# A graph attention kernel: edge features turned by DVE instead of TensorE, and eight output places in the last stage

## The chip, the cores and the metric

The kernel runs on one core of one Trainium2 chip. The metric is the device time of one execution in microseconds (us); lower is better. Engines carry the names of the profile: PE (TensorE), DVE (VectorE), ACT (ScalarE), POOL (GpSimd) and SP (SyncE).

## The reference

N = 12500 nodes with 96 features, 8 heads of 12, E = 412500 edges sorted by destination. Each edge has 96 features of its own.

```
q = x @ Wq + bq;  k = x @ Wk + bk;  v = x @ Wv + bv      # per node
e = edge_attr @ We + be                                  # per edge
score = k[src] * q[dst] / sqrt(12) * e                   # per edge, 96 wide
score = exp(clip(score summed over each head, -5, 5))    # per edge and head
wV = segment_sum(v[src] * score, dst);  Z = segment_sum(score, dst)
out = layernorm(x + wV / (Z + 1e-6))
```

## The kernel before, in words

The edges are taken in C = 806 chunks of 512 (CHUNK), each as G = 4 tiles of 128. There are four stages.

*Nodes.* 25 batches of 4 x 125 nodes: PE turns x and multiplies it, and the rows of k and v go to a table in DRAM, `kv_table`, 768 bytes a node; then 25 batches for q, stored in three bf16 parts in `q_table`, while DVE clears `accT`, which holds the sums of all nodes (L874). Tables of the destinations are turned on PE (L590) and copied by DVE (L850).

*Main stage.* Each engine runs a step of its own for each chunk, all in a loop written out eight or sixteen steps at a time, and they meet by counting semaphores only:
- POOL (L518 to L531) waits until the place of its ring is free (`msg_ready` of 8 chunks before, RING = 8) and issues 4 indirect gathers of `kv_table` rows (L527), whose row numbers come from `src_idx`.
- PE (L616 to L654), in step s: four turns of `ea` of chunk s (L635, edges by features into features by edges), with the products with `w_e` of chunk s - 2 between them (L637), the selection of query rows of chunk s - 2 (L644), and the sums of chunk s - 5 (L651); then it adds one to `pe_step`. Float32 products are issued as two passes each. Each product has two places in PSUM.
- ACT (L758 to L778) waits for `pe_step` s + 1: the exponential of the scores (L764), the copy of the turned edges to SBUF as `eaT` (L767), two operations that make the selection matrix `ohT` (L772, L775), and in every fourth step a load of source numbers (L340).
- DVE (L885 to L929) waits for `pe_step` a + 3: it multiplies gathered keys with queries (L898) and with e (L906), makes the matrix `oh` (L901), the messages (L910), which release POOL, the sums over heads (L917), adds to `accT` (L925) and clips the scores (L929).
- SP (L387 to L395), every 4 chunks, waits for `pe_step` (L390) and loads `ea` (L371), the destinations `dst_b` (L384) and four windows of queries (L379).

*Last stage.* 25 batches: PE turns the sums back (L703), DVE divides (L992, L995, L1000), POOL adds x (L549), DVE takes mean and variance (L1006, L1020), ACT the root, DVE its reciprocal (L1011) and the shift, minus mean times that (L1016), ACT applies both, SP stores. The finished rows have four places; the division (L1000) waits until the store of four batches before is done.

Of the kernel before, what the change touches and what calls it, by code (L numbers as in the profile page):

```python
# [20 lines left out]
PROJ_LAG = 2  # L21
SUM_LAG = 5
SEL = WIN * PARTS
SEL_READ = 106
RING = 8
HALF = RING // 2
IDX_RING = 16
# [14 lines left out]
def run_steps(engine, step, chunks, lag, round_values=None, from_round=0, unroll=RING, ahead=0):  # L42

    rounds = (chunks - 1 - ahead) // unroll
    if from_round == 0:
        for s in range(unroll):
            step(s, s, None)
# [8 lines left out]
def run_batches(engine, step, batches, lag, shift=0, after_first=None, before_last=None):  # L56

    rounds = (batches - 1 - shift) // 4
    for b in range(4 + shift):
        step(b, b % 4)
    if after_first is not None:
        after_first()
    with engine.Fori(1, rounds) as i:
        for u in range(4):
            step(i * 4 + u + shift, (u + shift) % 4)
    if before_last is not None:
        before_last()  # L70
    for b in range(rounds * 4 + shift, batches + lag):
        step(b, b % 4)


def gnn_kernel(nc, x, src, dst, edge_attr, Wq, bq, Wk, bk, We, be, Wv, bv, out):
# [14 lines left out]
    assert NQ * NJ == FULL and FULL == C - 1 and NP * TILES == N and DUP % G == 0  # L90
# [3 lines left out]
    assert CHUNK <= 512 and BATCH * max(DZ, NP) <= 512 and NQ * G <= 512 and BATCH % 2 == 0  # L94
# [7 lines left out]
    with ExitStack() as ctx:  # L102
# [3 lines left out]
        def sem(name):  # L106
# [13 lines left out]
        x_in = sb("x_in", [P, 4, BATCH, D])  # L120
        kv_out = sb("kv_out", [P, 4, BATCH, 2 * D])
        q_rest = sb("q_rest", [P, 2, BATCH, D])
        q_out = sb("q_out", [P, 4, BATCH, PARTS, D], BF16)
# [4 lines left out]
        spare = sb("spare", [P, 2 * 4 * BATCH * D + 2 * BATCH * D])  # L128
        dst_nat = spare[0:NQ, 0:NJ * CHUNK]
        dst16 = sb("dst16", [NQ, NJ * CHUNK], I16)  # L130
        dst16_end = sb("dst16_end", [1, CHUNK], I16)
        dst_end_row = sb("dst_end_row", [1, CHUNK], I32)
        dst_end = sb("dst_end", [P, G], I32)
        lohi = sb("lohi", [P, 4, NJ])
# [8 lines left out]
        rel = sb("rel", [P, C * G])  # L143

        ea = sb("ea", [P, RING, G, D])
# [3 lines left out]
        kv = sb("kv", [P, RING, G, 2 * D])  # L149
        eaT = sb("eaT", [DA, 2, CHUNK])  # L150
        away = sb("away", [SEL, CHUNK], BF16)
        ohT = sb("ohT", [SEL, 2, CHUNK], BF16)
        oh = sb("oh", [P, 2, G, WIN])
# [3 lines left out]
        msg = sb("msg", [P, 2, G, DZ])  # L157
# [5 lines left out]
        x_res, y = [spare[:, lo * BATCH * D:hi * BATCH * D].rearrange("p (u j d) -> p u j d", j=BATCH, d=D)  # L163
                    for lo, hi in ((0, 4), (4, 8))]
# [9 lines left out]
        eaT_ps, e_ps, q_ps, sum_ps = bank[0:2], bank[2:4], bank[4:6], bank[6:8]  # L174
# [5 lines left out]
        ones_ready = sem("ones_ready")  # L180
        w_kvq_in = sem("w_kvq_in")
        w_e_in = sem("w_e_in")
        dst_in = sem("dst_in")
        ends_in = sem("ends_in")
# [30 lines left out]
        ea_in = [sem(f"ea_in{i}") for i in range(2)]  # L215
        dst_b_in = [sem(f"dst_b_in{i}") for i in range(2)]
        q_win_in = [sem(f"q_win_in{i}") for i in range(RING)]
        src_idx_in = [sem(f"src_idx_in{i}") for i in range(IDX_RING // IDX_GROUP)]
# [4 lines left out]
        eaT_copied = sem("eaT_copied")  # L223
# [17 lines left out]
        f_eaT_copied = sem("f_eaT_copied")  # L241
# [27 lines left out]
        std_inverted = sem("std_inverted")  # L269
        coef_ready = sem("coef_ready")  # L270
        y_ready = sem("y_ready")
        y_stored = [sem(f"y_stored{i}") for i in range(4)]
# [53 lines left out]
        def wait_batch(engine, sems, b, u):  # L326

            engine.wait_ge(sems[u], 32 * (b // 4 + 1) if isinstance(b, int) else (b - u) * 8 + 32)
# [6 lines left out]
        def load_sources(engine, s, u):  # L335

            count = max(0, min(IDX_GROUP, C - s)) if isinstance(s, int) else IDX_GROUP
# [710 lines left out]
```

## Time and profile before

| | |
|---|---|
| median of 3 runs | 5354.8 us (5341.96 to 5366.8) |
| profiled execution: its time, its span | 5346.04 us, 5344.1 us |
| mean granted PE clock of it | 0.508 of full speed |
| busy share of the span: PE, DVE, ACT, POOL | 67%, 39%, 31%, 59% |
| main stage, last stage | about 235 to 5235 us, 5235 to 5344 us |

Busy time is time in which an instruction of the engine ran; the idle time before it is put down to what ended it. "remote" means that the releaser is not in the profile. PEld is PE's loading of weights, which overlaps its matmuls.

### The profile page before, as it was taken

Reading aid. Unit: us, or ns where it says so; the run is one execution under the profiler, and the core shown is the slowest. Engines: PE = TensorE matmul, PEld = TensorE weight load, DVE = VectorE, ACT = ScalarE, POOL = GpSimd, SP = SyncE. Lnnn points to the kernel's source line nnn. Section 1 sums busy time; section 2 is a strip of 40 time slices with the busy share of each in tenths; the row PEclk is TensorE's granted clock in tenths of the full one; section 3 lists DMA queues with packets and bytes.
Section 4 is the critical chain, followed back from the end, with each engine's and each line's share of the span. In section 5 each row is a group of like instructions: output and inputs, shape, how many; then the busy total and the mean of one; then the engine's idle time right before and its main releaser. Section 6 shows DMA issues by size and latency. Waiting matters only on the chain.

```text
span 5344.1 us, 72613 instructions
## 1 busy us (share of the span) xinstructions
PE 3563.7 (67%) x19972; PEld 3430.0 (64%) x19973; DVE 2070.6 (39%) x6072; ACT 1676.7 (31%) x3477; POOL 3154.1 (59%) x3274
## 2 busy tenths in 40 slices
PE   7666666666666666666666666666666666666665
PEld 6666666666666666666666666666666666666664
DVE  4433333333333333333333343333333333333336
ACT  4323232333323332323332332333322323333234
POOL 4566565565665656555656566655566565665662
PEclk7555555555555555555555555555555555555555
DMA  7344444444444444444444444444444444444443
GB/s 227 107 110 118 110 109 109 109 118 110 109 111 113 115 109 110 118 110 108 110 113 113 109 108 110 114 113 109 109 110 119 108 112 112 114 109 108 110 117 91
DMA packets 497769, 607.51 MB, mean 114 GB/s; under 512 B 256053, under 2 KB 420224, under 8 KB 497630
## 3 DMA queue, kind: packets, MB, share of 16 engines
q0 software_dynamic: 155200, 318.39, 22.6%
q1 hardware_dynamic: 233215, 281.36, 18.0%
q10 hardware_dynamic: 109330, 7.48, 1.5%
q8 instruction: 10, 0.16, 0.0%
q14 instruction: 14, 0.11, 0.0%
HBM read 584.51 MB, written 22.46 MB: 114 GB/s over the span
## 4 chain that ended last, share of the span: by engine, by line
PE 46%; issue 25%; another core or an unknown queue 18%; DVE 6%; DVEq 2%; ACT 1%; DMA 1%; SPq 1%; ACTq 0%; POOL 0%; POOLq 0%
PE bank L637 16%; PE bank L651 15%; PE bank L635 10%; PE bank L644 4%; DVE kqe L906 2%; DVE raw_score L917 1%; DVEq L298 1%; DVE oh L901 1%; DVE kqe L898 0%; ACT eaT L767 0%; DMA out_dram<-spare 0%; ACT spare L805 0%; DVE msg L910 0%; DVE accT L925 0%
## 5 line engine op out<-in xcount | busy, mean ns | idle before, releaser
L527 POOL DMA_INDIRECT kv<-kv_table,src_idx x3224 | 3104.5, 963 | 2090.2 <-DVE msg L910 1041.2
L637 PE MATMUL bank<-w_e,eaT 97*128 97x96 f32 x6448 | 1882.9, 392 | 216.6 <-issue 216.6
L635 PE MATMUL bank<-ident,ea 128*96 128x128 f32 x3224 | 1355.3, 421 | 958.3 <-issue 517.5
L637 PEld LDWEIGHTS bank<-w_e,eaT 97*128 97x128 f32 x6448 | 1776.7, 334 | 222.8 <-issue 221.9
L898 DVE TENSOR_TENSOR kqe<-kv,bank 128x384 f32<-128x384 f32 x806 | 446.6, 554 | 3179.6 <-remote 2432.5
L651 PE MATMUL bank<-oh,msg 128*104 128x32 f32 x6448 | 1284.8, 353 | 276.7 <-issue 273.5
L635 PEld LDWEIGHTS bank<-ident,ea 128*96 128x96 f32 x3224 | 806.0, 250 | 986.2 <-issue 515.0
L651 PEld LDWEIGHTS bank<-oh,msg 128*104 128x104 f32 x6448 | 1234.3, 289 | 269.0 <-issue 264.9
L764 ACT ACTIVATE msg<-score 128x32 f32<-128x32 f32 x806 | 184.8, 229 | 3523.9 <-remote 2569.5
L644 PEld LDWEIGHTS bank<-q_win,ohT 96*128 96x128 bf16 x3224 | 401.4, 155 | 338.8 <-issue 332.4
L644 PE MATMUL bank<-q_win,ohT 96*128 96x96 bf16 x3224 | 447.2, 279 | 245.5 <-issue 241.1
L772 ACT ACTIVATE away<-dst_b,minus_id 96x512 bf16<-96x512 int16 x806 | 581.1, 721 | 0.0
L775 ACT ACTIVATE ohT<-away 96x512 bf16<-96x512 bf16 x806 | 508.1, 630 | 25.5
L767 ACT COPY eaT<-bank 96x512 f32<-96x512 f32 x806 | 454.1, 563 | 4.9 <-PE bank L644 4.2
L910 DVE TENSOR_TENSOR msg<-kv,msg 128x384 f32<-128x384 f32 x806 | 443.3, 550 | 0.2 <-ACT msg L764 0.2
L906 DVE TENSOR_TENSOR kqe<-kqe,bank 128x384 f32<-128x384 f32 x806 | 440.1, 546 | 0.0
L917 DVE TENSOR_REDUCE raw_score<-kqe 128x32 f32<-128x384 f32 x806 | 438.1, 544 | 0.0
L901 DVE TENSOR_TENSOR oh<-iota,rel 128x128 f32<-128x128 f32 x806 | 230.7, 286 | 0.0
L929 DVE TENSOR_SCALAR score<-raw_score 128x32 f32<-128x32 f32 x806 | 185.4, 230 | 0.1
L925 DVE TENSOR_TENSOR accT<-bank,accT 104x32 f32 x806 | 144.3, 179 | 2.8 <-PE bank L651 2.3
L549 POOL TENSOR_TENSOR spare<-spare 125x384 f32<-125x384 f32 x25 | 25.0, 1000 | 77.6 <-DVE spare L1000 77.6
L703 PE MATMUL bank<-ident,accT 104*125 104x104 f32 x100 | 30.6, 464 | 41.5 <-DVE spare L1000 39.1
(78 smaller groups left out, 481.0 us busy)
## 6 DMA issues: line engine op xcount, KB each, us to landing
ea<-in_edge_attr_dram SPq DMA_DIRECT2D x201, 768.0 KB
dst_b<-dst_by_chunk SPq DMA_DIRECT2D x201, 384.0 KB
kv<-kv_table,src_idx POOLq DMA_INDIRECT x3224
q_win<-q_table SPq DMA_DIRECT2D x806, 19.9 KB
kv_table<-kv_out SPq DMA_DIRECT2D x25, 336.0 KB
q_table<-q_out SPq DMA_DIRECT2D x25, 252.0 KB
spare<-in_x_dram SPq DMA_DIRECT2D x25, 168.0 KB
out_dram<-spare SPq DMA_DIRECT2D x25, 168.0 KB
```

Of the source, the lines that this page charges most:

```text
L527: pool.indirect_dma_start(kv[:, slot, g, :], None, kv_dram[:, :], bass.IndirectOffsetOnAxis(ap=src_idx[:, u, g:g + 1], axis=0)).then_inc(k ...
L635: last = nc.tensor.transpose(eaT_ps[u % 2][0:D, g * P:(g + 1) * P], ea[:, u, g, :], ident[:, :])
L637: nc.tensor.matmul(e_ps[v % 2][:, g * D:(g + 1) * D], eaT[:, v % 2, g * P:(g + 1) * P], w_e[:, :], start=True, stop=True)
L644: last = nc.tensor.matmul(q_ps[v % 2][:, g * D:(g + 1) * D], sel[:, g, :], q_win[0:SEL, v, :], start=(g == 0), stop=(g == G - 1), skip_gro ...
L651: last = nc.tensor.matmul(sum_ps[w % 2][0:DZ, 0:WIN], msg[:, w % 2, g, :], oh[:, w % 2, g, :], start=(g == 0), stop=(g == G - 1))
L767: nc.scalar.copy(eaT[0:D, u % 2, :], eaT_ps[u % 2][0:D, :]).then_inc(eaT_copied, 1)
L772: nc.scalar.activation(away[:, :], dst_b[:, u % RING, :], ACT.Abs, bias=minus_id[:, bass.ds(s, 1)]).then_inc(away_done, 1)
L775: nc.scalar.activation(ohT[:, u % 2, :], away[:, :], ACT.Relu, bias=1.0, scale=-1.0).then_inc(ohT_built, 1)
L898: nc.vector.tensor_tensor(kqe[:, :, :], kv[:, ua, :, 0:D], q_ps[ua % 2][:, 0:G * D].rearrange("p (g d) -> p g d", g=G), ALU.mult).then_inc ...
L906: nc.vector.tensor_tensor(kqe[:, :, :], kqe[:, :, :], e_ps[ua % 2][:, 0:G * D].rearrange("p (g d) -> p g d", g=G), ALU.mult).then_inc(kqe_ ...
L910: nc.vector.tensor_tensor(msg[:, um % 2, :, 0:D].rearrange("p g (h d) -> p g h d", d=HD), kv[:, um, :, D:2 * D].rearrange("p g (h d) -> p ...
L917: nc.vector.tensor_reduce(raw_score[:, :], kqe[:, :, :].rearrange("p g (h d) -> p (g h) d", d=HD), AX_X, ALU.add).then_inc(heads_summed, 1)
```

## The change

Edge features. `ea` is no longer turned by PE and copied by ACT. A load of 4 chunks becomes three loads, one for each 32 of the 96 features. Each puts edge 32 b + i of its block b on partition i, so that 32 features of one edge (128 bytes in DRAM) are one piece. That is 2048 pieces for each of the three loads, where one load had 512 pieces of 1536 bytes. On DVE one instruction per chunk turns the 32x32 blocks of 96x512 into `eaT`. These loads have a ring of 16 chunks, are issued by ACT and go 15 chunks ahead. The order of edges inside a chunk changes with it, in all tables alike.

Pipeline. `eaT`, `ohT`, `oh`, `msg` and the PSUM results have four places (DEPTH = 4). PE's step s now works on chunk s for both products, and on chunk s - 5 for the sums. DVE's turn and ACT's `ohT` are made 4 steps ahead. DVE waits for `pe_step` a + 1.

Tables. All source numbers are loaded once and turned on PE (28 small turns) and copied by DVE to `src_tab`; ACT copies 4 chunks of them every fourth step in place of the load. The destination tables' turns are spread over the node batches. `dst_b` is loaded by ACT, x by SP, the numbers of the edges by POOL. In the query stage every second clearing of `accT` (12 of 25) is made by ACT.

Last stage. The finished rows have eight places. The shift is made by POOL in two operations of 125x4 (zero minus mean, times the reciprocal), behind its own addition of x.

The diff, cut to its core:

```diff
+        def load_edges(engine, s, g):
+
+            count = min(EA_GROUP, C - s) if isinstance(s, int) else EA_GROUP
             whole = count - 1 if isinstance(s, int) and s + count == C else count
-            if whole > 0:
-                engine.dma_start(src_idx[:, u:u + whole, :], src[bass.ds(s * CHUNK, whole * CHUNK)].rearrange(
-                    "(c p g) -> p c g", p=P, g=G)).then_inc(src_idx_in[u // IDX_GROUP], 16)
-            if whole < count:
-                engine.dma_start(src_idx[:, u + whole, :], src[E - CHUNK:E].rearrange(
-                    "(p g) -> p g", g=G)).then_inc(src_idx_in[u // IDX_GROUP], 16)
+            parts = [(s * CHUNK, g * EA_GROUP, whole)] + ([(E - CHUNK, g * EA_GROUP + whole, 1)] if whole < count else [])
+            for edge, slot, chunks in parts:
+                for k in range(0, D, SQ):
+                    engine.dma_start(ea[k:k + SQ, slot:slot + chunks, :].rearrange("i c (b f) -> i (c b) f", f=SQ),
+                                     edge_attr[bass.ds(edge, chunks * CHUNK), k:k + SQ].rearrange(
+                                         "(b i) f -> i b f", i=SQ)).then_inc(ea_in[g], 16)
...
             def half_round(s, h, bases):
 
-                sp.wait_ge(pe_step, s - HALF + PROJ_LAG)
+                sp.wait_ge(pe_step, s - HALF)
                 sp.sem_inc(loads_allowed, 1)
-                load_edges(s, h)
-                load_destinations(s, h)
...
+            def finish(b, u):
+                if not isinstance(b, int) or b < BATCHES:
+                    pool.wait_ge(y_attended, b + 1)
+                    wait_batch(pool, x_res_in, b, u % 4)
+                    nc.gpsimd.tensor_tensor(y[0:NP, u, :, :], y[0:NP, u, :, :], x_res[0:NP, u % 4, :, :], ALU.add).then_inc(res_added, 1)
+                if not isinstance(b, int) or b >= 2:
+                    w = u % 2
+                    pool.wait_ge(std_inverted, b - 1)
+                    nc.gpsimd.tensor_tensor(shift[0:NP, w, :], zero[0:NP, 0:1].to_broadcast((NP, BATCH)), mean_var[0:NP, w, :, 0],
+                                            ALU.subtract).then_inc(mean_negated, 1)
+                    pool.wait_ge(mean_negated, b - 1)
+                    nc.gpsimd.tensor_tensor(shift[0:NP, w, :], shift[0:NP, w, :], std_inv[0:NP, w, :], ALU.mult).then_inc(coef_ready, 1)
+
+            run_batches(pool, finish, BATCHES, 2, 0, OUT_RING)
...
-                if projecting:
-                    pe.wait_ge(eaT_copied, c + 1)
-                    at_least(pe, kqe_done, c - 1)
-                for g in range(G):
-                    if turning:
-                        last = nc.tensor.transpose(eaT_ps[u % 2][0:D, g * P:(g + 1) * P], ea[:, u, g, :], ident[:, :])
...
+                if projecting:
+
+                    pe.wait_ge(ea_turned, s + 1)
+                    for g in range(G):
+                        nc.tensor.matmul(e_ps[v][:, g * D:(g + 1) * D], eaT[:, v, g * P:(g + 1) * P],
...
+            def copy_sources(s, u):
+
+                count = max(0, min(IDX_GROUP, C - s)) if isinstance(s, int) else IDX_GROUP
+                if count > 0:
+                    nc.scalar.copy(src_idx[:, u:u + count, :], src_tab[:, bass.ds(s * G, count * G)].rearrange(
+                        "p (c g) -> p c g", g=G)).then_inc(src_copied, count)
...
-                    nc.scalar.copy(eaT[0:D, u % 2, :], eaT_ps[u % 2][0:D, :]).then_inc(eaT_copied, 1)
...
+                    if w % HALF == HALF - 1 and (not isinstance(t, int) or t + HALF + 1 < C):
+                        load_destinations(act, t + HALF + 1, w // HALF)
+
+                if u % IDX_GROUP == 0 and (not isinstance(s, int) or s >= 0):
+                    copy_sources(s + IDX_AHEAD, (u + IDX_AHEAD) % IDX_RING)
+
+                if u % EA_GROUP == 1 and (not isinstance(s, int) or 0 <= s and s + EA_AHEAD < C):
+                    act.wait_ge(ea_turned, s + EA_AHEAD - EA_RING + EA_GROUP)
+                    load_edges(act, s + EA_AHEAD, (u + EA_AHEAD) % EA_RING // EA_GROUP)
...
-                dve.wait_ge(pe_step, a + PROJ_LAG + 1)
...
+                    dve.wait_ge(pe_step, a + 1)
...
+                    w = (u + DEPTH) % EA_RING
+                    if w % EA_GROUP == 0:
+                        landed_edges(dve, t, w)
+                    nc.vector.transpose(eaT[0:D, v, :], ea[:, w, :]).then_inc(ea_turned, 1)
...
-                    if not isinstance(b, int) or b >= 4:
-                        wait_batch(dve, y_stored, b - 4, u)
+                    if not isinstance(b, int) or b >= OUT_RING:
+                        wait_batch(dve, y_stored, b - OUT_RING, u)
...
-                    nc.vector.scalar_tensor_tensor(shift[0:NP, w, :], mean_var[0:NP, w, :, 0], -1.0, std_inv[0:NP, w, :],
-                                                   ALU.mult, ALU.mult).then_inc(coef_ready, 1)
```

PE, one step of the main loop. Before, the turn into one PSUM bank alternates with the product into another:

```order
L631 REGISTER_ALU
L635 MATMUL bank1<-ident,ea 96x128
L637 MATMUL bank3<-w_e,eaT 128x96
L635 MATMUL bank1<-ident,ea 96x128
L637 MATMUL bank3<-w_e,eaT 128x96
L635 MATMUL bank1<-ident,ea 96x128
L637 MATMUL bank3<-w_e,eaT 128x96
L635 MATMUL bank1<-ident,ea 96x128
L637 MATMUL bank3<-w_e,eaT 128x96
L644 MATMUL bank5<-q_win,ohT 128x96 x4
L651 MATMUL bank6<-oh,msg 104x32 x4
```

After, two steps; the turns are gone and each chunk has its own bank out of four:

```order
L663 REGISTER_ALU
L665 MATMUL bank1<-w_e,eaT 128x96 x4
L670 MATMUL bank5<-q_win,ohT 128x96 x4
L678 MATMUL bank1<-oh,msg 104x32 x4
L663 REGISTER_ALU
L665 MATMUL bank2<-w_e,eaT 128x96 x4
L670 MATMUL bank6<-q_win,ohT 128x96 x4
L678 MATMUL bank2<-oh,msg 104x32 x4
```

The four L635 rows left the step, and the sums (L678) share a bank with the products of e (L665).

DVE, one step of the main loop. Before, the step ends with the clipping of the scores:

```order
L898 TENSOR_TENSOR kqe<-kv,bank5 128x384
L901 TENSOR_TENSOR oh<-iota,rel 128x128
L906 TENSOR_TENSOR kqe<-kqe,bank3 128x384
L910 TENSOR_TENSOR msg<-kv,msg 128x4x96
L917 TENSOR_REDUCE raw_score<-kqe 128x32
L922 TENSOR_LOAD base_tab
L922 ISA x2
L925 ISA
L925 TENSOR_TENSOR accT<-bank6,accT 104x32
L929 TENSOR_SCALAR score<-raw_score 128x32
```

After, with the lines of the changed kernel:

```order
L944 TENSOR_TENSOR kqe<-kv_mem,bank4 128x384
L947 TENSOR_TENSOR oh<-iota,rel 128x128
L952 TENSOR_TENSOR kqe<-kqe,bank0 128x384
L956 TENSOR_TENSOR msg<-kv_mem,msg 128x4x96
L963 TENSOR_REDUCE raw_score<-kqe 128x32
L968 TENSOR_LOAD base_tab
L968 ISA x2
L971 ISA
L971 TENSOR_TENSOR accT<-bank0,accT 104x32
L975 TENSOR_SCALAR score<-raw_score 128x32
L980 STREAM_TRANSPOSE eaT<-ea_mem 96x512
```

One row was added, the turn at the step's end, for the chunk four steps ahead.

ACT, in the main loop. Before, the step with the load of source numbers at its end:

```order
L764 ACTIVATE msg<-score 128x4x8
L767 COPY eaT<-bank0 96x512
L285 ISA
L772 ISA
L772 ACTIVATE away<-dst_b,minus_id 96x512
L775 ACTIVATE ohT<-away 96x512
L340 ISA
L340 DMA src_idx<-in_src_dram 128x4x4
L760 REGISTER_ALU
```

After, the steps around the two kinds of loads (`ea_mem` holds the edge features, `src_tab` the source numbers):

```order
L376 DMA dst_b<-dst_by_chunk 96x2048
L791 ACTIVATE msg<-score 128x4x8
L798 ACTIVATE away<-dst_b,minus_id 96x512
L801 ACTIVATE ohT<-away 96x512
L757 CAST src_idx<-src_tab 128x16
L791 ACTIVATE msg<-score 128x4x8
L798 ACTIVATE away<-dst_b,minus_id 96x512
L801 ACTIVATE ohT<-away 96x512
L361 DMA ea_mem<-in_edge_attr_96_dram 32x64x32 x3
```

The copy of `eaT` and the source load left ACT; a small copy, one load of destinations and three loads of edge features per four steps came to it.

## Rows read from the trace of the kernel before

**Rows 1.** Stretch of the main stage: PE, PEld, DVE, ACT, POOL busy (count), clock, DMA share, GB/s.
```profile
2235.00:3235.00 1000.00, 666.51 (x3754) 644.78 (x3754) 377.85 (x1092) 304.70 (x624) 601.55 (x626) 0.50 0.41 111
```

**Rows 2.** Groups by line, main stage: busy, mean ns, idle time before and releasers.
```profile
L527 POOL DMA_INDIRECT kv<-kv_table,src_idx x3132 | 3011.9, 962 | 1988.9 <-DVE msg L910 1000.0 <-issue 988.8
```

**Rows 3.** Timeline of GpSimd: start, duration, operation, idle time before.
```profile
2483.27 0.95 POOL L527 DMA_INDIRECT kv<-kv_table,src_idx  x1 [4.83 <-DVE msg L910]
...
2508.68 0.95 POOL L527 DMA_INDIRECT kv<-kv_table,src_idx  x1 [4.67 <-DVE msg L910]
2509.93 1.14 POOL L527 DMA_INDIRECT kv<-kv_table,src_idx  x1 [0.30 <-issue]
```

**Rows 4.** Timeline of DVE, the same 26 us.
```profile
2486.41 0.55 DVE L898 TENSOR_TENSOR kqe<-kv,bank 128x384 f32<-128x384 f32 x1 [0.75 <-PE bank L651]
...
2496.78 0.56 DVE L898 TENSOR_TENSOR kqe<-kv,bank 128x384 f32<-128x384 f32 x1 [8.00 <-remote]
...
2506.18 0.55 DVE L898 TENSOR_TENSOR kqe<-kv,bank 128x384 f32<-128x384 f32 x1 [7.01 <-remote]
...
2508.56 0.55 DVE L898 TENSOR_TENSOR kqe<-kv,bank 128x384 f32<-128x384 f32 x1
...
2511.77 0.55 DVE L898 TENSOR_TENSOR kqe<-kv,bank 128x384 f32<-128x384 f32 x1 [0.69 <-PE bank L651]
```

**Rows 5.** Chain of waits in order of time: start, length, what.
```profile
2486.38 0.24 PE bank L635
...
2486.99 0.21 PE bank L635
...
2490.43 0.24 PE bank L635
...
2494.48 3.68 issue
...
2501.39 1.79 issue
```

**Rows 6.** Page, costliest groups: who waits for "remote".
```profile
L898 DVE TENSOR_TENSOR kqe<-kv,bank 128x384 f32<-128x384 f32 x806 | 446.6, 554 | 3179.6 <-remote 2432.5
...
L764 ACT ACTIVATE msg<-score 128x32 f32<-128x32 f32 x806 | 184.8, 229 | 3523.9 <-remote 2569.5
```

**Rows 7.** Waits of SyncE's queue: total us, times, longest.
```profile
SPq L390 <- remote: 2135.8, 130, 23.9
```

**Rows 8.** Timeline of all engines around the first gather.
```profile
67.64 2.08 SPq L384 DMA_DIRECT2D dst_b<-dst_by_chunk  x2
...
71.30 1.05 POOL L527 DMA_INDIRECT kv<-kv_table,src_idx  x1 [32.23 <-DMA kv_table<-kv_out]
...
80.28 7.03 PE L601 MATMUL bank<-w_kvq,accT 97*125 97x96 f32 x32 [7.03 <-issue]
```

**Rows 9.** Page, costliest groups: the rows that the edits touch.
```profile
L527 POOL DMA_INDIRECT kv<-kv_table,src_idx x3224 | 3104.5, 963 | 2090.2 <-DVE msg L910 1041.2
...
L635 PE MATMUL bank<-ident,ea 128*96 128x128 f32 x3224 | 1355.3, 421 | 958.3 <-issue 517.5
...
L549 POOL TENSOR_TENSOR spare<-spare 125x384 f32<-125x384 f32 x25 | 25.0, 1000 | 77.6 <-DVE spare L1000 77.6
```

**Rows 10.** Timeline of DVE in the last stage.
```profile
5285.17 0.56 DVE L1000 TENSOR_TENSOR spare<-bank,z_inv 125x384 f32<-125x384 f32 x1 [1.01 <-DMA out_dram<-spare]
...
5287.70 0.56 DVE L1000 TENSOR_TENSOR spare<-bank,z_inv 125x384 f32<-125x384 f32 x1
...
5289.08 0.28 DVE L1016 SCALAR_TENSOR_TENSOR shift<-mean_var,std_inv 125x4 f32<-125x4 f32 x1
```

**Rows 11.** Waits in the last stage: total us, times, longest.
```profile
DVE spare L1000 <- DMA out_dram<-spare: 14.0, 16, 1.8
```

**Rows 12.** Page, DMA queues: packets, bytes, share of 16 engines' span.
```profile
q1 hardware_dynamic: 233215, 281.36, 18.0%
q10 hardware_dynamic: 109330, 7.48, 1.5%
```

More of the change, by code:

```diff
@@ L39, in at_least, with run_steps @@
         engine.wait_ge(sem, value)
-def run_steps(engine, step, chunks, lag, round_values=None, from_round=0, unroll=RING, ahead=0):
+def run_steps(engine, step, chunks, lag, round_values=None, lead=0, unroll=RING, ahead=0):
     rounds = (chunks - 1 - ahead) // unroll
-    if from_round == 0:
-        for s in range(unroll):
-            step(s, s, None)
+    for s in range(-lead, unroll):
+        step(s, s % unroll, None)
     with engine.Fori(1, rounds) as i:
@@ L53, in run_steps, with run_batches @@
         step(s, s % unroll, None)
[L56 to L65, printed above, removed]
-    with engine.Fori(1, rounds) as i:
[L67 to L72, printed above, removed]
+def run_batches(engine, step, batches, lag, shift=0, unroll=4):
+    rounds = (batches - 1 - shift) // unroll
+    for b in range(unroll + shift):
+        step(b, b % unroll)
+    with engine.Fori(1, rounds) as i:
+        for u in range(unroll):
+            step(i * unroll + u + shift, (u + shift) % unroll)
+    for b in range(rounds * unroll + shift, batches + lag):
+        step(b, b % unroll)
 def gnn_kernel(nc, x, src, dst, edge_attr, Wq, bq, Wk, bk, We, be, Wv, bv, out):
@@ L326, in wait_batch @@
         def wait_batch(engine, sems, b, u):
-            engine.wait_ge(sems[u], 32 * (b // 4 + 1) if isinstance(b, int) else (b - u) * 8 + 32)
+            ring = len(sems)
+            engine.wait_ge(sems[u], 32 * (b // ring + 1) if isinstance(b, int) else (b - u) * (32 // ring) + 32)
         def within(node):
@@ L415, in _ @@
                 load_queries(u, first_bases[u])
+            for g in range(2, EA_RING // EA_GROUP):
+                load_edges(sp, g * EA_GROUP, g)
             rounds = (C - 1) // RING
@@ L748, in query_batch @@
                         "p (j d) -> p j d", d=D)).then_inc(q_first, 1)
+                    if u % 2 == 1:
+                        nc.scalar.copy(accT[:, bass.ds(b * (BATCH * NP), BATCH * NP)],
+                                       zero[:, 0:1].to_broadcast((P, BATCH * NP))).then_inc(acc_zeroed, 1)
                 if not isinstance(b, int) or b >= 1:
@@ new lines, in step @@
+                if not isinstance(s, int) or t < C:
+                    w = (u + DEPTH) % RING
+                    if w % HALF == 0:
+                        landed_half(act, t, w)
+                    at_least(act, ohT_built, t)
+                    nc.scalar.activation(away[:, :], dst_b[:, w, :], ACT.Abs,
+                                         bias=minus_id[:, bass.ds(t, 1)]).then_inc(away_done, 1)
+                    act.wait_ge(away_done, t + 1)
+                    nc.scalar.activation(ohT[:, v, :], away[:, :], ACT.Relu, bias=1.0, scale=-1.0).then_inc(ohT_built, 1)
+                    if w % HALF == HALF - 1 and (not isinstance(t, int) or t + HALF + 1 < C):
+                        load_destinations(act, t + HALF + 1, w // HALF)
```

340 lines of the change are left out of this document (178 added, 162 removed).

## The prediction

> **What bounds the kernel now.** I read the page's busy times first, then the table of stretches, then GpSimd's and TensorE's rows in one stretch of the main stage. No engine is full: in each 1000 us of the main stage PE works some 667 us, GpSimd 601, DVE 378, ACT 305, and the DMA engines 42% [rows 1]. The main stage holds 5000 of the 5344.1 us of the span. So the reader should look for what waits in a circle. GpSimd issues four gathers for each chunk of 512 edges. Between 235 and 5235 us it issued 3132 of them (783 chunks): 3011.9 us of work, 988.8 us of its own gaps, 1000.0 us of waiting for DVE's message step, which gives back the gather's place [rows 2]. That is (3011.9 + 988.8)/783 = 5.11 us of its own and 1.28 us of waiting, together 6.39 us a chunk. It goes in bursts: 16 gathers at 1.25 us from 2483.27 to 2504.0, then 4.67 us of waiting; the burst before was ended by 4.83 us [rows 3]. The period is 25.4 us for 4 chunks (2483.27 to 2508.68), 6.35 each.
>
> Why is DVE late? Its own step is short: from 2506.18 to the next at 2508.56 are 2.38 us without a pause [rows 4]. PE's step is 4.05 us (2486.38 to 2490.43) when nothing stops it [rows 5]. DVE's first operation waits for a finished PE step. PE's steps end at 2490.43 and 2494.48 [rows 5], yet DVE starts on them at 2496.78 and 2506.18, after 8.00 and 7.01 us whose releaser the profile gives as "remote" [rows 4]. ACT and SyncE, waiting for the same count, show the same word: 2569.5 us on ACT, 2432.5 on DVE [rows 6], 2135.8 on SyncE, which waits for nothing else at that place [rows 7]. In the pause after 2506 DVE takes steps at 2506.18, 2508.56 and 2511.77, and the last waits 0.69 us for PE's own matmul, by name [rows 4]. PE itself stands 3.68 and 1.79 us with nothing to wait for that the profile shows ("issue"), and the second of these lies between two matmuls of one step, right where gathers are being issued [rows 3, 5], and an "issue" stall of 7.03 us up to 80.28 follows on the first gather of the run at 71.30 [rows 8]. I therefore read it like this: **while GpSimd issues gathers without pause, a PE step gets through to the others only about every 9.9 us ((2506.18 − 2486.41)/2); in the pause they get through at PE's own pace.** This is inferred from coincidence in time, not shown, and it is the weakest step here.
>
> A sum tests it. If n chunks go by per pause, the period is T = 5.11n + 4.8. The open part of it is 5.6 us (2506.18 to 2511.77) and passes 2 steps; the rest, 5.11n + 4.8 − 5.6, passes one per 9.9 us. n = (5.11n − 0.8)/9.9 + 2 gives n = 3.97 and 6.32 us a chunk. The trace has 4 and 6.39. The model is 1% short, so I scale what it gives by 6.39/6.32.
>
> **The change, part by part.**
> *The turn leaves PE.* 3224 turns (1355.3 us of matmul [rows 9]) and 806 ACT copies go. In a step the turns are 0.24 + 3 × 0.21 = 0.87 us of the 4.05 [rows 5], so a free step is 3.18 us. The open part, which passed 2 steps, then passes 2 × 4.05/3.18 = 2.55 at best and 2.0 at worst; I take 2.3, about the middle. The blocked pace is the disputed size. If it goes by the number of PE instructions (matmuls with their loads: 24 pairs in a step before, 20 after), it is 9.9 × 20/24 = 8.25 us; by PE's time, 9.9 × 3.18/4.05 = 7.8; if it is a property of the release alone it stays 9.9. I take 8.25, the middle of the three: n = (5.11n − 0.8)/8.25 + 2.3 gives n = 5.79, T = 34.4, 5.94 us a chunk, scaled 6.01. That is 0.38 less than 6.39, times 806: **−305 us**. With 7.8: n = 6.37, 5.93 scaled, −370. With 9.9: n = 4.59, 6.23 scaled, −130.
> *The turn comes to DVE.* One 96x512 turn of 32x32 blocks per step. No row shows one. The nearest is a 128x384 product in 0.55 us [rows 4], which is the lower bound; scaled to 512 columns it is 0.73, the upper. I take 0.6: DVE's step becomes 2.38 + 0.6 = 3.0 us against 6.0 a chunk, hidden in its waiting. Without that cover it costs 0.6 × 806 = 480 us. DVE also meets GpSimd oftener: the gather that starts at 2509.93, while DVE works, takes 1.14 instead of 0.95 us [rows 3, 4]. One such meeting more per chunk is +0.19 × 806 = +153 us on GpSimd's own pace, zero is the other end; I take zero, because 1.14 comes at one gather in 16 although DVE works through most of them.
> *Edge loads.* One load of 512 pieces of 1536 bytes per 4 chunks becomes three loads with 6144 pieces of 128 bytes, issued by ACT 15 chunks ahead instead of by SyncE 4 ahead. I cost it at nothing in the forecast: the DMA engines are 42% busy [rows 1], and 15 chunks are 90 us. What it costs without this cover is rival B. On ACT each issue stands in front of the next exponential; three at the 1.04 us of a dst_b issue (2.08 for two [rows 8]) and one dst_b are 4.2 us per 4 chunks. ACT works 304.7 of 1000 us [rows 1], 7.8 per 4 chunks with the copies that go: 12 of 24 us at most, hidden. The small source load every fourth step becomes an ACT copy of 128x16, no more than the 229 ns of its 128x32 exponential [rows 6], hidden. SyncE keeps only the query windows.
> *Four places instead of two* in PSUM and for the turned operands let PE run 4 steps ahead of DVE rather than 2. In the model nothing is gained, since the rate of release binds; if it is a delay of release and not a rate, all is gained (rival A).
> *Before the main stage.* 28 more turns at 0.21 us start to start [rows 5] are 5.9 us of PE; half of the clearing of accT leaves DVE for ACT, which I count as nothing, both being in the same chain. GpSimd waits 32.23 us for table stores before its first gather [rows 8], which covers the conversion of the sources. I take +5 us; ends −5, and +40 if the first loads of 128-byte pieces (16 × 1536 × 14.6 ns/16 = 22 us, price below) land late.
> *Last stage.* A batch takes 2.53 us (5285.17 to 5287.70) where DVE waits for nothing, and the one before waited 1.01 us for a store [rows 10]. These waits are 14.0 us in 16 cases [rows 11]; eight places take them away. The shift is one DVE operation of 0.28 us a batch [rows 10], 7 us in all, of which I count 5, since such operations overlap. On GpSimd two operations of 125x4 follow the residual's 1000 ns [rows 9]; below 500 ns each they fit into the 2.53 us, at 1000 ns each GpSimd needs 3.0 and binds (+12 us). I take −14 − 5 + 3 = **−16**; ends −21 and +12.
> The sum: 5346.04 (the profiled run: 2 us around its span, and 9 us or 0.2% under the median, which I leave aside) − 305 + 5 − 16 = **5030 us**.
>
> **Rivals.**
> *A: GpSimd alone binds.* If a PE step is released late but several can be under way, four places cover the 6.35 and 11.7 us that DVE stands behind PE [rows 4, 5], and all 1041.2 us of GpSimd's waiting [rows 9] go: 5346 − 1041 − 11 = **4294 us**. For it: PE had stopped at 2494.48 because the turned operand was not copied, that is, for want of places. Against it: the single matmuls 1.2 to 1.8 us apart, which more places don't cure.
> *B, the other side: pieces of 128 bytes cost transfer time that lies in line with the gathers.* The small queue paid 1.5% × 5344.1 × 16/109330 = 11.7 ns for a piece of 68 bytes, the queue of SyncE and ACT 18.0% × 5344.1 × 16/233215 = 66 ns for 1206 bytes [rows 12]. On the line through both, 128 bytes cost 14.6 ns and 1536 bytes 81.7. Per 4 chunks: 6144 × 14.6/16 = 5.6 us, against 512 × 81.7/16 = 2.6 and 0.4 for the source load. That is 2.6 us more, 0.65 a chunk if none is hidden: 6.01 + 0.65 − 6.39 = +0.27, times 806 = +218; 5346 + 218 − 11 = **5553 us**. It decides from 11.8 ns a piece on (where the 0.38 us a chunk are used up); at 17 ns it gives 5740. If it isn't in line, only full engines bind: 6.01 × 16 / 1536 is 63 ns a piece less what others use, 42% of it, so above some 36 ns. For it: gathers and edge pieces meet in the same 16 engines, and a gather must have landed before DVE can use it. Against it: 58% of these engines' time is free [rows 1], and the loads are 15 chunks early.
> By the Trainium skill, "DMA: Bandwidth & Descriptors", Specifications, a transfer reaches line rate from 512 bytes on, and below that the engine does a read-modify-write. The two queues' rows show a price falling with size down to 68 bytes, which does not agree with it. An estimate by the page, at the 33 ns that the same line gives for 512 bytes, is 12.6 us per 4 chunks and a time near 7000 us if it is all in line, and no change of my sum if it is not.
> *C: no change.* If DVE's last release of each burst stays what ends GpSimd's pause, 4 chunks a period as now, only the ends of the kernel move: **5335 us**.
>
> **Chances.** Forecast 0.38 (own range 4900 to 5220, from −370 and −130 and the ends of the small terms), A 0.22 (4290 to 4800), B 0.33 (5400 and up, half of it below 5740), C 0.07. The range from 4290 to 5740 leaves out about 0.2. A measurement here tells about 0.5% (5328 to 5382) from no change. Faster: 0.38 + 0.22 = 0.60; same 0.07; slower 0.33.
>
> **What would show it.** Right: a PE step near 3.2 us; five to seven chunks between GpSimd's pauses; its waiting for DVE down from 1041 to some 730 us; "remote" waits still there; DVE's turn at 0.5 to 0.7 us; stores no longer waited for in the last stage. A: no wait for DVE's message left. B: waits for edge loads on DVE's turn, a queue share well above 18%, or gathers that land late. Wrong altogether: a clock that leaves its 0.50 [rows 1], DVE or ACT as the last to arrive at every step, or a gather longer than 0.96 us.

## The result and the profile after

The changed kernel takes 5284.2 us (median of 4, 5282.8 to 5284.7), the kernel before 5360.8 (4 runs, 5342.0 to 5368.2). The ratio is 0.986 (95% interval 0.983 to 0.989), a gain of 1.4%. I had forecast 5030 us, 6% less. The direction was right and the size four times too large. Only the widest range, 4290 to 5740 us, holds the value: it lies above the forecast's own range (4900 to 5220), below that of B, and 51 us below C's 5335.

The spans of the two profiles differ by 63.1 us (5344.1 and 5281.0). The first and the last step of DVE's main loop split them. Timeline of DVE in the kernel before, its first step and its last:

```profile
135.89 0.56 DVE L898 TENSOR_TENSOR kqe<-kv,bank 128x384 f32<-128x384 f32 x1 [7.70 <-issue]
...
5253.25 0.56 DVE L898 TENSOR_TENSOR kqe<-kv,bank 128x384 f32<-128x384 f32 x1 [1.13 <-PE bank L651]
```

The same of the changed kernel:

```profile
162.98 0.56 DVE L944 TENSOR_TENSOR kqe<-kv_mem,bank 128x384 f32<-128x384 f32 x1 [5.83 <-PE bank L670]
...
5206.10 0.56 DVE L944 TENSOR_TENSOR kqe<-kv_mem,bank 128x384 f32<-128x384 f32 x1 [0.89 <-PE bank L678]
```

Up to the first step it takes 27.1 us longer, the main loop 5043.1 instead of 5117.4 us (74 less), and what follows 74.9 instead of 90.9 us (16.0 less).

The page of the changed kernel, costliest groups (out<-in, count, busy us and mean ns, idle before and releaser); they answer to [rows 6] and [rows 9]:

```profile
L553 POOL DMA_INDIRECT kv_mem<-kv_table,src_idx x3224 | 3117.8, 967 | 2037.2 <-DVE msg L956 1043.3
...
L665 PE MATMUL bank<-w_e,eaT 97*128 97x96 f32 x6448 | 1663.8, 429 | 328.1 <-issue 321.8
...
L944 DVE TENSOR_TENSOR kqe<-kv_mem,bank 128x384 f32<-128x384 f32 x806 | 427.8, 531 | 2677.1 <-remote 2133.4
L791 ACT ACTIVATE msg<-score 128x32 f32<-128x32 f32 x806 | 184.9, 229 | 3798.9 <-remote 2633.6
...
L980 DVE STREAM_TRANSPOSE eaT<-ea_mem 96x512 f32<-96x512 f32 x806 | 564.3, 700 | 0.0
```

GpSimd's waits before, then after (total us, times, longest):

```profile
POOL kv L527 <- DVE msg L910: 1041.2, 273, 25.4
POOL kv L527 <- issue: 1016.8, 2950, 2.6
```
```profile
POOL kv_mem L553 <- DVE msg L956: 1043.3, 234, 36.8
POOL kv_mem L553 <- issue: 944.5, 2989, 2.8
```

GpSimd still waits 1043.3 us for DVE's message step, in fewer and longer waits than before. The remote waits are there too, 2133.4 and 2633.6 us. Of GpSimd's idle time in the main stage only that by "issue" became smaller, by 72 us, which is about as much as the main loop gained. DVE's turn takes 700 ns and hides as forecast.

### The profile page after: what moved, and what is told of

Same layout as the page of the kernel before. It is cut to its first block, busy times and chain, and to the rows that moved or that the text cites. A ratio compares the mean times of both kernels' runs of the same rounds, so it can differ in the third digit from the quotient of the medians.

```text
span 5281.0 us, 65022 instructions
## 1 busy us (share of the span) xinstructions
PE 3108.9 (59%) x16776; PEld 3038.4 (58%) x16777; DVE 2471.5 (47%) x6851; ACT 1338.4 (25%) x2885; POOL 3184.4 (60%) x3332
## 3 DMA queue, kind: packets, MB, share of 16 engines
q10 hardware_dynamic: 1245734, 233.93, 23.6%
## 4 chain that ended last, share of the span: by engine, by line
PE 55%; issue 40%; DVE 1%; another core or an unknown queue 1%; DMA 1%; SPq 1%; ACT 0%; DVEq 0%; POOL 0%; ACTq 0%; POOLq 0%
PE bank L665 28%; PE bank L678 21%; PE bank L670 5%; DMA kv_mem<-in_x_dram 1%; PE bank L613 0%; DVE y_stats L1060 0%; SPq L361 0%; DMA q_table<-ea_mem 0%; SPq L395 0%; DVE kqe L952 0%; DVE raw_score L963 0%; SPq L428 0%; SPq L381 0%; DVE z_inv L1049 0%
## 5 line engine op out<-in xcount | busy, mean ns | idle before, releaser
L553 POOL DMA_INDIRECT kv_mem<-kv_table,src_idx x3224 | 3117.8, 967 | 2037.2 <-DVE msg L956 1043.3
L678 PE MATMUL bank<-oh,msg 128*104 128x32 f32 x6448 | 1302.8, 337 | 1611.2 <-issue 1610.5
L678 PEld LDWEIGHTS bank<-oh,msg 128*104 128x104 f32 x6448 | 1282.1, 285 | 1586.5 <-issue 1585.4
L665 PE MATMUL bank<-w_e,eaT 97*128 97x96 f32 x6448 | 1663.8, 429 | 328.1 <-issue 321.8
L665 PEld LDWEIGHTS bank<-w_e,eaT 97*128 97x128 f32 x6448 | 1494.7, 330 | 400.6 <-issue 399.0
L944 DVE TENSOR_TENSOR kqe<-kv_mem,bank 128x384 f32<-128x384 f32 x806 | 427.8, 531 | 2677.1 <-remote 2133.4
L791 ACT ACTIVATE msg<-score 128x32 f32<-128x32 f32 x806 | 184.9, 229 | 3798.9 <-remote 2633.6
L980 DVE STREAM_TRANSPOSE eaT<-ea_mem 96x512 f32<-96x512 f32 x806 | 564.3, 700 | 0.0
L956 DVE TENSOR_TENSOR msg<-kv_mem,msg 128x384 f32<-128x384 f32 x806 | 441.7, 548 | 16.9 <-issue 12.9
L639 PE MATMUL bank<-w_kvq,accT 97*125 97x96 f32 x200 | 37.5, 373 | 30.2 <-issue 17.8
L639 PEld LDWEIGHTS bank<-w_kvq,accT 97*125 97x125 f32 x200 | 36.1, 285 | 31.7 <-issue 19.4
L576 POOL TENSOR_TENSOR kv_mem<-kv_mem,spare 125x384 f32<-125x384 f32 x25 | 25.0, 999 | 44.5 <-DVE kv_mem L1054 44.5
```

The costliest lines, as they stand in the source:

```text
L553: pool.indirect_dma_start(kv[:, slot, g, :], None, kv_dram[:, :], bass.IndirectOffsetOnAxis(ap=src_idx[:, u, g:g + 1], axis=0)).then_inc(k ...
L665: nc.tensor.matmul(e_ps[v][:, g * D:(g + 1) * D], eaT[:, v, g * P:(g + 1) * P], w_e[:, :], start=True, stop=True)
L678: last = nc.tensor.matmul(sum_ps[v], msg[:, w, g, :], oh[:, w, g, :], start=(g == 0), stop=(g == G - 1), skip_group_check=True)
L944: nc.vector.tensor_tensor(kqe[:, :, :], kv[:, ua, :, 0:D], q_ps[v][:, 0:G * D].rearrange("p (g d) -> p g d", g=G), ALU.mult).then_inc(kq_d ...
L956: nc.vector.tensor_tensor(msg[:, um % DEPTH, :, 0:D].rearrange("p g (h d) -> p g h d", d=HD), kv[:, um, :, D:2 * D].rearrange("p g (h d) - ...
L980: nc.vector.transpose(eaT[0:D, v, :], ea[:, w, :]).then_inc(ea_turned, 1)
```

## The experiments

Eighteen kernels ran, on five occasions. One thing has to be said ahead of them. The kernel before, run each time on the same chip beside them, took 5358 us (beside e1 to e4), 4259 (e5 to e8), 5354 (e9 to e12), 5350 (e13 to e16) and 4252 us (e17 and e18). The second and the fifth time the chip was in a state that I had not known of: in the traces of the kernels that ran there, DVE and ACT have no remote waits left. The chips were listed as 11, 9, 7, 6 and again 7, so it isn't a fixed property of a chip: number 7 showed both. I call the first state *held* (before at about 5354 us) and the second *free* (about 4255). Within an occasion it didn't change: all 7 to 17 executions of the kernel before are of one kind. My prediction and its result are both of the held state, and a kernel is compared only with kernels of its own occasion or state. What makes a chip held is open. The changed kernel itself never ran in the free state; e7 and e8, which are it with a little more work, took 4281 and 4293 us there, where the kernel before took 4259. That the change gains anything there is not shown.

**What holds PE: the gathers themselves.** e1 takes them from GpSimd, e2 leaves half of them out.

```diff
 # e1: SyncE, every 4 chunks, behind its wait
+                sp.wait_ge(msg_ready, s - HALF)
+                    sp.dma_start(kv[:, slot, g, :], kv_dram[(slot * G + g) * P:(slot * G + g + 1) * P, :]).then_inc(kv_in[slot], 16)
-                    pool.indirect_dma_start(kv[:, slot, g, :], None, kv_dram[:, :],
...
 # e2
-                for g in range(G):
+                for g in range(2):
...
```

> The changed kernel, but GpSimd issues no gathers in the main stage: SyncE loads the same bytes of the node table as four plain loads of 128 rows a chunk into the same places (always the same rows, so the scores are of other nodes). Theory 1, gathers being issued hold back PE's finished steps: the remote waits of DVE and ACT go, and the main stage runs at the pace of the longest step, DVE's 3.1 us or PE's 3.2, so about 5284 - (6.3 - 3.4) x 806 = 2950 us, at most 3500. Theory 2, the place ring and the landing of node rows set the pace (DVE waits for the data): the loads are as many bytes and descriptors, and come only four chunks ahead, so the time stays above 4500. Theory 3, the pieces of 128 bytes load the DMA engines so that everything that lands is late: they are still there, so above 4500 too.

> The changed kernel with two of the four gathers of a chunk left out (the other half of the places holds zeros). GpSimd's own floor falls from 5.1 to 2.5 us a chunk. Theory 1: the main stage is then bound by DVE or PE, 3.1 to 4.2 us a chunk, total 2750 to 3600 us. Theory 3 (128-byte pieces): little changes, above 4800. If time per gather is conserved, 6.3/4 = 1.57 us each, it is 3.15 us a chunk and indistinguishable from DVE's bound: then the remote waits tell.

Held state, by the kernel before beside them: 3552 us (my upper end was 3500) and 3051 us, one run each. In e1 as many bytes still move, though always of the same rows, and the remote waits are gone. What binds there most is SyncE, which has 16 more loads to issue per four chunks (the chain that ended last gives its issuing 32%). In e2 PE is the bound. Stretches of e2 (PE, PEld, DVE, ACT, POOL busy, clock, DMA share, GB/s) and its waits:

```profile
1235.00:2235.00 1000.00, 997.34 (x5708) 994.16 (x5707) 836.73 (x2290) 435.16 (x930) 545.51 (x573) 0.50 0.68 146
```
```profile
ACT msg L794 <- remote: 248.6, 79, 5.4
...
DVE kqe L947 <- remote: 99.8, 65, 3.8
```

PE is busy 997 of 1000 us at the same clock of 0.50, with 3.50 us a chunk, and ACT's remote waits fall from 2634 to 249 us. Two gathers every 3.5 us hold hardly anybody. e2 reads scattered rows as the kernel does, so the rows of e1 are not what did it. So theory 1 stands: sustained gathers hold the others.

**What does not matter: pieces, ring, bytes, rows, source loads.**

```diff
 # e3: one run of 8192 bytes a partition
-                    engine.dma_start(ea[k:k + SQ, slot:slot + chunks, :].rearrange("i c (b f) -> i (c b) f", f=SQ),
+                    engine.dma_start(ea[k:k + SQ, slot:slot + chunks, :].rearrange("i c e -> i (c e)"),
...
 # e4, with KV_RING = 4
-                at_least(pool, msg_ready, s - RING + 1)
+                at_least(pool, msg_ready, s - KV_RING + 1)
...
 # e6, e12: half rows            # e15: half as many rows
+                    pool.indirect_dma_start(kv[:, slot, g, 0:D], None, kv_dram[:, :],
+                    pool.indirect_dma_start(kv[0:64, slot, g, :], None, kv_dram[:, :],
...
 # e8, e14: SyncE, every 4 chunks
+                sp.dma_start(src_x[:, h, 0:count, :], src[bass.ds(s * CHUNK, count * CHUNK)].rearrange(
...
```

> The changed kernel with the three loads of edge features kept, as many bytes to the same places, but each partition gets one run of 8192 bytes (so the features are not those of the edges): 96 pieces instead of 6144 per four chunks. Theory 3, the small pieces ate the gain: 100 to 350 us faster than the changed kernel, 4930 to 5180. Theory 1, the gathers' issue sets the pace whatever else: within 25 us of 5284.

> The changed kernel with four places for gathered rows instead of eight. Theory 1 as a rate (a fixed time per gather while others are held back): within 50 us of 5284. Theory 2 (the depth of the ring and the landing of the gathers set the pace): with half the depth clearly slower, 5800 us or more.

> The changed kernel with gathers of half rows (384 bytes, the value half of the places holds zeros), as in e6, which took 4371 us beside 4259 of the kernel before. On a chip where the kernel before takes 5358 us: a limit per gather or row leaves it at 5284 within 60 us; a limit on bytes brings it down to GpSimd's own pace, about 4370.

> The changed kernel with as many gathers, but of 64 rows instead of 128 (the other half of the partitions holds zeros). Halving the bytes left the time at 5300 us (e12), so the limit is per gather or per row. Per row, or per row descriptor that GpSimd writes: the holding goes and GpSimd's own issuing binds, 4370 us or less. Per gather: within 60 us of 5284.

> The changed kernel plus the source loads of the kernel before (512 pieces of 16 bytes per four chunks, into a tile that nobody reads), as in e8. Where the kernel before takes 5354 us: 5330 or more if the main stage's gain came from leaving out these loads, within 15 us of 5284 if not. Where it takes 4259: 4293 again.

Held state, medians: e3 5297 us (5290 to 5305), e4 5288 (5286 to 5299), e12 5300 (5293 to 5302), e15 5302 (5292 to 5312), e14 5285 (5278 to 5293). All lie within 18 us of 5284, and none is faster than the changed kernel beyond its noise. Rival B is out: 96 pieces instead of 6144 per four chunks gained nothing. Queues of the changed kernel and of e3 (packets, MB, share of 16 engines' span):

```profile
q10 hardware_dynamic: 1245734, 233.93, 23.6%
```
```profile
q10 hardware_dynamic: 51398, 233.93, 16.6%
```

A piece of 128 bytes costs 23.6% x 5281.0 x 16/1245734 = 16.0 ns of an engine, near the 14.6 that I had read from [rows 12]. The Trainium skill ("DMA: Bandwidth & Descriptors", Specifications) has the line rate only from 512 bytes on. The rate agrees: the queue's share falls from 23.6% to 16.6% for the same bytes. But no one waits for these loads (DVE's turn has no idle time before it), so it costs no time here. The ring may be half as deep, and the gathers half as heavy in bytes or in rows: what counts is how many gathers there are and, by e16 below, how closely they follow on one another.

e6 and e8 are the same kernels as e12 and e14 in the free state:

> The changed kernel with gathers of half rows (the 96 key features of 192 columns, 384 bytes; the value half of the places holds zeros). As many gathers and rows, half the bytes. If the limit is per gather or per row: within 60 us of 5284. If it is bytes: GpSimd's own 5.1 us a chunk binds, about 4330 us.

> The changed kernel plus the source loads of the kernel before (512 pieces of 16 bytes per four chunks, by SyncE, into a tile that nobody reads). If these took part in the limit: most of the main stage's 0.09 us a chunk comes back, 5330 to 5360. If not: within 15 us of 5284.

They took 4371 and 4293 us, where the kernel before took 4259. e6's expectation meant the held state, so 4371 doesn't tell bytes from gathers there; e12 does.

**PE's work matters, a little.** e7 (free) and e13 (held) put four turns a step back on PE; nobody uses their results.

```diff
                     for g in range(G):
+                        nc.tensor.transpose(q_ps[v][0:D, G * D:G * D + P], ident[:, 0:D], ident[:, :])
                         nc.tensor.matmul(e_ps[v][:, g * D:(g + 1) * D], eaT[:, v, g * P:(g + 1) * P],
```

> The changed kernel with four turns of 128x96 per step put back on PE between the products (of the identity, into unused PSUM columns; nobody waits for them). Theory of my prediction (the held pace of PE goes by its instructions, or by its work): it gives back most of the gain of the main stage, 5340 us or more. Theory 4: PE's own work does not matter, within 15 us of 5284.

> The changed kernel with four turns of 128x96 per step put back on PE (of the identity, into unused PSUM columns), as in e7, whose chip did not show the holding. Where the kernel before takes 5354 us: if the held pace of PE goes by its instructions or its work (the step of my prediction with 8.25 instead of 9.9 us), most of the main stage's gain of some 70 us goes, 5335 us or more. If PE's work does not matter, within 15 us of 5284. Where the kernel before takes 4259: 4281 again, no answer.

e7: 4281 us, and GpSimd has hardly a wait left:

```profile
L553 POOL DMA_INDIRECT kv_mem<-kv_table,src_idx x3224 | 3111.6, 965 | 1052.9 <-issue 951.4 <-DVE msg L957 52.1 <-DMA kv_table<-kv_mem 49.3
```

e13: 5340 us (median of 10, 5332 to 5356). That is 55 above e14, which ran beside it and took what the changed kernel takes. GpSimd waits 1096.2 us for DVE:

```profile
POOL kv_mem L553 <- DVE msg L957: 1096.2, 276, 41.1
POOL kv_mem L553 <- issue: 946.0, 2947, 2.8
```

So in the held state PE's four turns are worth 55/806 = 0.07 us a chunk. I had forecast 0.38. The expectation of e13 took 5335 us or more as a sign that the held pace goes by PE's work; the time is there, but the table in the next section shows that the held steps did not become slower with the turns.

**The changed kernel again, and its last stage.**

```diff
 # e10: four output places, the shift back on DVE
-OUT_RING = 8
+OUT_RING = 4
...
```

> The changed kernel itself, since the kernel before took 5358 us beside the first four experiments and 4259 us beside the next four, on another chip, without remote waits. Theory 5: what I read as a rule of this kernel (PE's steps are held while gathers are issued) is a property of one chip or its surroundings; where it is absent, GpSimd's own issuing binds at 5.07 us a chunk and the change is worth no more than its ends. If the kernel before takes about 4260 here: the changed kernel within 25 us of it, 4235 to 4285. If it takes about 5358: 5284, within 15 us.

> The changed kernel with its last stage as before: four output places, the shift on DVE. By the profiles (109 us against about 95) it is 10 to 16 us slower than the changed kernel on either chip, all of it after the main stage. Rival: the stores hide it, within 3 us.

Held state: 5284.4 us (ratio 0.987, 0.985 to 0.989) and 5299.1 (5294.7 to 5305.9). The last stage is worth 14.7 us, against 16 forecast.

**Gathers spaced evenly.** e5 (free), e11 and e16 (held), e17 (free), and the kernel before with the same in e18 (free):

```diff
                                             ).then_inc(kv_in[slot], 16)
+                    at_least(pool, paced, s * G + g)
+                    pool.sem_inc(pace_seen, 1)
+                    nc.gpsimd.memset(pace[:, :], 0.0).then_inc(paced, 1)
 # pace is 128x200 in e5 and e11, 128x232 in e17, 128x264 in e16 and e18
```

> The changed kernel with a small GpSimd operation (clearing 128x200) behind each gather, so that gathers come every 1.6 to 1.7 us evenly instead of 16 at 1.25 us and a pause. Theory 4, formed after the first four kernels: something behind the gathers takes one only every 1.57 us (6.30/4), the surplus piles up for some 8 us and then PE is held until it drains. Then the remote waits of DVE and ACT fall below a quarter of 2133 and 2634 us, GpSimd no longer waits for DVE, and the time is what the spacing gives: 3224 x the spacing + 220, so 5280 at 1.57 and 5600 at 1.67. Theory 1 in its first form (any gather being issued holds PE, gaps let it go) gives fewer remote waits too, but a time that keeps PE's holding: above 5284 by more than the spacing explains.

> The changed kernel with the clearing of 128x200 behind each gather, as in e5, which took 4830 us (1.43 us a gather) where the kernel before took 4259. On a chip where the kernel before takes 5358 us: if something takes gathers only every 1.57 us (theory 4), the even spacing of 1.43 us does not help, 5284 within 40 us. If it is the interplay of bursts and PE's steps, even gaps let PE's steps through, and the time falls to that of the spacing, about 4830 us. Where the kernel before takes 4259: 4830 again.

> The changed kernel with a clearing of 128x264 behind each gather, so a gather every 1.50 us. With 1.43 us it took 5129, which is (5129 - 220)/3224 = 1.52 us a gather, so the holding was nearly gone. If what takes the gathers has a capacity of one per 1.52 us or less when they come evenly: 1.50 x 3224 + 230 = 5070 to 5150 us and the remote waits below half of 2080 and 2625 us. If PE's holding follows each gather whatever the spacing: 5250 or more.

> The changed kernel with a clearing of 128x232 behind each gather, a gather every 1.43 us, between e11 (1.40 us, 5129 us, remote waits 2625 on ACT) and e16 (1.46 us, 4975 us, remote waits 164). If the holding begins at a threshold, the time lies on one side: about 3224 x 1.43 + 240 = 4860 us with few remote waits, or above 5000 with many. If it fades evenly: about 5050 with some 1400 us of remote waits. Where the kernel before takes 4259: 4870.

> The kernel before with nothing changed but a clearing of 128x264 behind each gather (1.46 us). If the spacing alone ends the holding, the change isn't needed for it: 3224 x 1.46 + 260, about 4970 to 5010 us. If PE's extra work (the turns, which gave back 55 of the main stage's 70 us in e13) puts the old kernel above the limit at this spacing: 5100 to 5300. Where the kernel before takes 4259: 4980.

Held state: e11 5129 us (ratio 0.958, 0.956 to 0.961), **e16 4975 us (ratio 0.931, 0.926 to 0.935)**. That is the best version where the gathers hold PE, 309 us below the changed kernel, by slowing GpSimd down. The clearings took 284 ns (128x200) and 338 ns (128x264), less than I had reckoned, so the gathers came closer together than the expectations of e5 and e16 say. Timelines of GpSimd in e11 and e16, then the waits of both:

```profile
2481.17 0.96 POOL L556 DMA_INDIRECT kv_mem<-kv_table,src_idx  x1 [0.17 <-issue]
...
2482.57 0.96 POOL L556 DMA_INDIRECT kv_mem<-kv_table,src_idx  x1 [0.17 <-issue]
```
```profile
2481.25 0.96 POOL L556 DMA_INDIRECT kv_mem<-kv_table,src_idx  x1 [0.17 <-issue]
...
2482.71 0.96 POOL L556 DMA_INDIRECT kv_mem<-kv_table,src_idx  x1 [0.17 <-issue]
```
```profile
ACT msg L797 <- remote: 2625.2, 341, 15.0
...
POOL kv_mem L556 <- DVE msg L962: 360.1, 113, 17.4
```
```profile
DVE kqe L950 <- DMA kv_mem<-kv_table,src_idx: 1574.9, 572, 5.7
...
ACT msg L797 <- remote: 164.5, 37, 7.9
```

A gather every 1.40 us leaves ACT's remote waits at 2625.2 us; every 1.46 us they are 164.5, and DVE waits for node rows to land, by name. Somewhere between, for evenly spaced gathers, lies the point at which most of the holding sets in. Theory 4 (one gather per 1.57 us at most) is out: e16 takes one every 1.46 us and is hardly held, and e11, from which it expected no gain (5284 within 40 us), gained 155 us with its remote waits still there. e17 and e18, made to find that point and to see whether the kernel before needs the change at all, fell in the free state: 4901 and 4921 us beside 4252. There they only cost their spacing (so did e5, 4830, the same kernel as e11). Both questions stay open.

## Why the prediction was right in direction and wrong in size

*What bounds the kernel* held. The step that I called the weakest, PE's steps held while GpSimd issues gathers without pause, is shown by e2 (half the gathers, hardly any holding) and e16 (as many, spaced, hardly any holding). How a gather holds the others is not shown.

*The blocked pace of 8.25 us* is the step that failed. I let the pace at which held steps get through fall with PE's instructions, from 9.9 us, and took 305 us from it; the main loop gave 74, or 0.09 a chunk. Counted over the whole traces, the held steps became longer instead. A step is here the time from the end of PE's last sum product of a chunk to that of the next, and I call it held when it is longer than 5 us:

| | before | changed | changed again (e9) | turns back (e13) |
|---|---|---|---|---|
| steps up to 5 us: number, mean us | 492, 4.10 | 546, 3.52 | 536, 3.55 | 512, 4.08 |
| longer steps: number, mean us | 313, 9.91 | 259, 12.03 | 269, 11.64 | 293, 10.27 |

Without the turns a held step takes 12.0 instead of 9.9 us, and with them back it takes 10.3. Fewer are held, but together they last about as long as before, some 3100 us. With a limit of 4.4 or of 6 us instead of 5 the held steps lengthen all the same (9.5 to 11.7, 10.3 to 12.4 us), but their sums move by up to 70 us either way, so how the 74 us divide between held and free steps stays open. I had expected five to seven chunks between GpSimd's pauses. Waits of over 2 us for DVE's message came 215 times before and 196 times after, so every 15 and every 16.4 gathers, still about four chunks. Why a held step stretches when PE has less to do stays open.

*The free step* was mis-sized too: it is 3.49 us and not 3.18. The products with `w_e` take 429 ns each where they follow on one another; between turns they took 392, in the kernel before and again in e13 (groups of its main stage):

```profile
L637 PE MATMUL bank<-w_e,eaT 97*128 97x96 f32 x6448 | 1882.9, 392 | 216.6 <-issue 216.6
```
```profile
L666 PE MATMUL bank<-w_e,eaT 97*128 97x96 f32 x6288 | 1879.3, 392 | 528.3 <-issue 524.2
```

Chain of waits of the changed kernel, in order of time:

```profile
2484.24 1.81 PE bank L665 x8
2486.05 0.32 PE bank L670 x4
2486.37 1.36 PE bank L678 x8
2487.73 1.81 PE bank L665 x8
...
2497.80 1.92 issue
2499.93 1.22 issue
2501.36 1.92 issue
```

One free step runs from 2484.24 to 2487.73; further down stand 1.92, 1.22 and 1.92 us of a held one. My formula can't be saved by a better number. With 9.9, the end of the range that I had kept as a bound, and 2.16 passes (the middle of 2 and 2 x 4.05/3.49) it gives −76 us and meets the measured 74, but that is luck: with the measured 12.0 it gives a loss of 89 us. Nor has it a place for e11 and e16, since it doesn't know of the spacing. What the runs say in any case is that in the held state a chunk takes 5043.1/805 = 6.26 us, so a gather some 1.57 us instead of the 1.25 of a burst, whether ring, bytes or rows are halved, and that PE's turns add 0.07 us a chunk.

*GpSimd's gaps* ("issue") fell by 72 us and its wait for DVE stayed, where I had expected the wait to fall. e14 shows that the left-out source loads are not the cause. e13's turns raise the wait by 53 us and the gaps by 2, so the turns don't explain the gaps either. Why the gaps fell stays open.

*Before the main stage* I took +5 us with +40 as the end. It was 27.1 us, by DVE's first step. GpSimd's wait for the node table grew from 32.23 us [rows 8] to 49.4, and PE waits 20.8 us for x:

```profile
POOL kv_mem L553 <- DMA kv_table<-kv_mem: 49.4, 1, 49.4
...
PE bank L599 <- DMA kv_mem<-in_x_dram: 20.8, 11, 5.0
```

Its first gather comes at 88.56 us, 17 later. The stores of the node table now stand on SyncE behind the loads of x, three batches late, and the loads of x behind its waits. That this order causes both is my reading; it wasn't tried. The other part of the 27 us is the holding again, which I had reckoned with in the main stage only: while the first 32 gathers go out, ACT waits 17.3 us for "remote" in the query stage. With 16 first gathers (e4), with spaced ones (e16) and in the free state (e7) this wait is gone and DVE's first step comes at 149.2, 148.9 and 149.9 us instead of 163.0.

*Last stage*: −16 forecast, −16.0 in the profiles (from DVE's last step to the end, 90.9 and 74.9 us), 14.7 by e10 against e9. This term was right.

*The rivals.* A, GpSimd alone binds at 4294 us, has a time close to what the free state shows (4281 in e7), but its condition, four places, is not what brings it: the kernel before, with two, takes 4259 there. More places did not free the held kernel, as I had argued from the single matmuls. B fell with e3. C, no change (5335), was nearer than my forecast: the pause of GpSimd stayed after some 16 gathers. One reading was slightly off: [rows 1] has the DMA engines 41% busy, not 42%, which moves nothing.

## What to carry to other kernels

When an engine waits for a finished step of another long after that step ended, look at what the issuing engine of the gathers does meanwhile, and try to space the gathers before rebuilding the pipeline: 0.2 us of idle work behind each was worth 309 us here, the whole change 76. And run the kernel before beside each experiment: on two other occasions it took 4255 instead of 5354 us. There the clearing of 128x264, which in e16 together with the change had gained 7%, cost the kernel before 16% (e18).

## What the runs showed of the hardware

- The same kernel (the one before) has two levels on these chips, about 5354 and 4255 us, at nearly the same granted clock (0.508 and 0.510 of full speed), and one chip number showed both.
- With evenly spaced gathers in the held state, PE's stalled matmuls start in step with the gathers. Timeline of e11, GpSimd's gathers and PE's single sum products:

```profile
2499.82 0.96 POOL L556 DMA_INDIRECT kv_mem<-kv_table,src_idx  x1 [0.17 <-issue]
...
2500.17 0.21 PE L684 MATMUL bank<-oh,msg 128*104 128x32 f32 x1 [0.99 <-issue]
...
2501.22 0.96 POOL L556 DMA_INDIRECT kv_mem<-kv_table,src_idx  x1 [0.17 <-issue]
2501.62 0.21 PE L684 MATMUL bank<-oh,msg 128*104 128x32 f32 x1 [1.25 <-issue]
```

  PE's products begin 0.35 and 0.40 us after a gather begins, one for each. Over the whole of e11, 778 of the 1011 matmuls before which PE stood over 0.8 us begin 0.3 to 0.8 us after the start of a gather. In the changed kernel, without the spacing, such matmuls are spread over the whole interval.
- A gather costs GpSimd the same 0.96 us with rows of 768 or 384 bytes (963 ns in e12), and 0.92 us with 64 rows instead of 128 (918 ns in e15).
- One turn of 96x512 by DVE in 32x32 blocks takes 700 ns.
